# An LSTM mixture behind windowed attention: the cell's work a gate unit later, halves stored as pairs, and the output projection with features on partitions

## What is computed

```python
h = tok(x)                                   # embedding (89 columns) beside a short-time spectrum (39)
h = h + attn(layernorm(h)) @ W_out + b_out   # 8 heads of 16; 64 summary tokens and windows of 17
n = layernorm(h)
top2 = top_k(n @ router_w + router_b, 2)     # weights: a softmax over the two
# every expert e is an LSTM over the 16 steps, for both choices k and all 512 tokens:
gates = (mask[k, e] * n) @ Wi[e] + hid @ Wh[e] + b[e]      # i, f, g, o
c = sigmoid(f) * c + sigmoid(i) * tanh(g)
hid = sigmoid(o) * tanh(c)
out = h + sum over k, e of mask[k, e] * weight[k] * (hid @ Wo[e] + bo[e])
```

## Time and profile before

| what | value |
|---|---|
| time, median of 3 runs | 1915.93 us (1915.46 to 1918.11) |
| the profiled execution | 1918.11 us |
| its span, first to last instruction | 1916.3 us |
| PE busy | 1729.1 us, 90% |
| DVE busy | 1559.5 us, 81% |
| ACT busy | 991.9 us, 52% |
| POOL busy | 65.2 us, 3% |
| granted TensorE clock, mean | 0.970 |

### The profile page before, as it was taken

One profiled execution on the slowest core, in us unless ns is written; L12 is line 12 of the kernel. 1 busy time (PEld: TensorE's weight loads), 2 busy tenths in 40 slices (PEclk: granted clock), 3 DMA queues, 4 the chain that ended last, 5 costly groups with the idle time before them and its releaser, 6 DMA issues.

```text
span 1916.3 us, 25885 instructions
## 1 busy us (share of the span) xinstructions
PE 1729.1 (90%) x9898; PEld 837.6 (44%) x9898; DVE 1559.5 (81%) x2433; ACT 991.9 (52%) x1114; POOL 65.2 (3%) x42
## 2 busy tenths in 40 slices
PE   3457799999999999999999999999999999999998
PEld 2223344444444444444444444444444444444443
DVE  2649698897988889798898988889898888979865
ACT  3234554646555555645545455455555555564544
POOL 1000000000000000000000000000000000000000
PEclk9668899999999999999999999999999999999999
DMA  3113241413314132232313224151331413223221
GB/s 114 20 41 74 57 67 46 77 37 67 63 49 74 39 70 52 52 70 51 67 45 69 51 57 67 44 80 37 63 66 46 76 37 71 53 50 67 55 61 36
DMA packets 318594, 110.95 MB, mean 58 GB/s; under 512 B 240331, under 2 KB 299581, under 8 KB 318471
## 3 DMA queue, kind: packets, MB, share of 16 engines
q1 hardware_dynamic: 202758, 101.96, 23.9%
q10 hardware_dynamic: 115712, 7.34, 3.8%
HBM read 89.84 MB, written 4.74 MB: 49 GB/s over the span
## 4 chain that ended last, share of the span: by engine, by line
PE 40%; DVE 33%; DMA 8%; issue 7%; ACT 5%; ACTq 4%; SPq 1%; POOL 0%; DVEq 0%
PE gates L506 25%; ACTq L619 4%; DVE C L1017 4%; DVE tmp L1007 4%; DMA masks<-mask_scratch 3%; DVE tmp L1013 3%; DMA prod<-in_x_ids 3%; DVE xm L985 3%; PE yp L512 3%; DVE Hs L997 3%; DVE tmp L1028 3%; DVE xn L795 2%; PE FA L447 2%; ACT tmp L655 2%; PE FA L459 2%
## 5 line engine op out<-in xcount | busy, mean ns | idle before, releaser
L655 ACT ACTIVATE tmp<-gates,bias_sb 128x1024 f32<-128x1024 f32 x504 | 557.5, 1109 | 558.6 <-PE gates L506 496.1
L506 PE MATMUL gates<-xm,wi_sb 128*128 128x512 f16 x3024 | 747.3, 384 | 46.2 <-ACT tmp L655 31.0
L506 PE MATMUL gates<-Hs,wh_sb 128*128 128x512 f16 x2880 | 704.4, 381 | 0.0
L506 PEld LDWEIGHTS gates<-xm,wi_sb 128*128 128x128 f16 x3024 | 290.3, 99 | 435.3 <-issue 105.1
L506 PEld LDWEIGHTS gates<-Hs,wh_sb 128*128 128x128 f16 x2880 | 283.2, 98 | 344.3 <-issue 8.0
L662 ACT ACTIVATE tmp<-C 128x1024 f32<-128x1024 f32 x128 | 135.2, 1057 | 226.4 <-DVE C L1017 223.2
L992 DVE SCALAR_TENSOR_TENSOR tmp<-tmp 128x1024 f32<-128x1024 f32 x128 | 155.9, 1218 | 71.8 <-ACT tmp L662 71.8
L1007 DVE SCALAR_TENSOR_TENSOR tmp<-tmp 128x1024 f32<-128x1024 f32 x120 | 144.9, 1208 | 46.4 <-ACT tmp L655 44.9
L985 DVE TENSOR_TENSOR xm<-xs,masks 128x2048 f16<-128x2048 f16 x128 | 155.2, 1212 | 32.7 <-DMA masks<-mask_scratch 32.7
L997 DVE SCALAR_TENSOR_TENSOR Hs<-tmp,Hs 128x1024 f16<-128x1024 f32 x120 | 146.4, 1220 | 37.7 <-ACT Hs L666 36.7
L1013 DVE SCALAR_TENSOR_TENSOR tmp<-tmp,C 128x1024 f32<-128x1024 f32 x120 | 146.4, 1220 | 14.4 <-ACT tmp L655 14.0
(11 more groups left out here) (155 smaller groups left out, 1218.9 us busy)
## 6 DMA issues: line engine op xcount, KB each, us to landing
masks<-mask_scratch SPq DMA_DIRECT2D x128, 256.0 KB, 5.0
roww<-mw_scratch SPq DMA_DIRECT2D x128, 256.0 KB, 4.0
rowk<-mask_scratch SPq DMA_DIRECT2D x128, 128.0 KB, 3.0
diag<-pr SPq DMA_DIRECT2D x64, 112.0 KB, 4.3
diag<-vwin ACTq DMA_DIRECT2D x64, 112.0 KB, 4.8
out_dram<-h SPq DMA_DIRECT2D x16, 256.0 KB, 3.7
C<-in_wi SPq DMA_DIRECT2D x1, 2048.0 KB, 10.9
C<-in_wh SPq DMA_DIRECT2D x1, 2048.0 KB, 15.6
```

The source lines that it names most:

```text
L506: last = mm(gates[:, slot, k * SEQ:(k + 1) * SEQ], w, v, start=(i < K), stop=(i >= len(seq) - K))
L655: A(tmp[:, gate_at(gate, e), :], gates[:, (n - 1) % 2, :], ACT.Tanh, bias=bias_sb[:, e, gate:gate + 1], scale=UNSCALE).then_inc(s_tanh, 1)
```

## The change

**Cell work a unit later.** `cell(e)` moves to g = 0 of the following expert, with `cell_tanh` at the same g = 0 (behind the tanh of I), `hidden` to the end of g = 1, `split_hi` to g = 2, `hidden_lo` and `chosen` to g = 3, `input_part` to g = 2. `unit_y` and the bias of y stand at g = 1 instead of g = 0. To let this be, `tmp` has eight planes in place of seven (two for F, two for O), and the product of `chosen` goes to the second half of the O plane instead of a tile `z32`, so that its wait for the last `unit_y` goes and the tanh of O waits for `unit_y` instead. The last cell and cell tanh stand after the loop.

**Pairs of halves.** In `qz`, `vhl`, `vwin` and `diag`, the high and low half of an element stand beside each other. The DMAs move 32-bit elements, DVE transposes v once as 32-bit elements, and the products read the diag tile with a step of two halves.

**Projection.** One product of `wout` with the 512 columns of `attn` at t = 21 (features on partitions), a copy on ACT at t = 21 that adds the bias, and four transposes on PE at t = 22. `moments2`, `xn2`, `x2T`, `logits`, `choice`, `weights` and `maskT` each stand one unit later. `SP_AT`, `MASKS_AT` and `XM_AT` don't change; SP's store of the output stands at t = 10 instead of 9.

The diff, without declarations and setup:

```diff
...
     SP_AT = dict(ids=0, qbd=6, rows=28)
-    PE_AT = dict(emb=1, xT=3, qkv=4, summary=7, window=8, feature=14, values=18, proj=21, x2T=23,
-         logits=24, maskT=27)
-    ACT_AT = dict(h=1, xT=3, qkv=4, split=5, summary=9, window=11, vz=9, pr_hi=15, feature=16, x2T=23,
-          choice=25, maskT=27)
+    PE_AT = dict(emb=1, xT=3, qkv=4, summary=7, window=8, feature=14, values=18, proj=21, projT=22,
+         x2T=24, logits=25, maskT=28)
+    ACT_AT = dict(h=1, xT=3, qkv=4, split=5, summary=9, window=11, vz=9, pr_hi=15, feature=16, proj=21, x2T=24,
+          choice=26, maskT=28)
     DVE_AT = dict(onehot=0, moments=1, xn=2, pw=5, q_lo=5, kv_lo=6, v_win=7, w_max=8, s_max=9, s_sub=10, w_sum=11,
           w_out=12, s_sum=13, s_norm=14, f_max=15, p_lo=16, p_T=16, f_sum=17, f_part=18, attn=19,
-          moments2=21, xn2=22, x_lo=24, choice1=25, choice2=25, weights=26)
+          moments2=22, xn2=23, x_lo=25, choice1=26, choice2=26, weights=27)
     MASKS_AT = 29
...
 Hs = sb("Hs", [P, E, 2, K * SEQ], f16)
-tmp = sb("tmp", [P, 7, K * SEQ])
+tmp = sb("tmp", [P, 8, K * SEQ])
 masks = sb("masks", [P, 2, K, SEQ], f16)
...
 roww = sb("roww", [P, 2, SEQ])
-z32 = sb("z32", [P, SEQ])
...
 oW = sb("oW", [P, NW])
-diag = sb("diag", [P, 2, NBLK, NG, 2 * DH], f16)
+diag = sb("diag", [P, NBLK, NG, 2 * DH])
 vwin = sb("vwin", [P, NBLK * 32])
...
 wT = rows[WT0:WT0 + E, :]
-qz = pr[:, :].bitcast(f16).rearrange("p (v j c q) -> p v j c q", v=2, j=NBLK, c=2)
+qz = pr[:, :].bitcast(f16).rearrange("p (j c q v) -> p j c q v", j=NBLK, c=2, v=2)
...
 pr16, prT16 = pair16(pr[:, :], NBLK * KB), pair16(prT[:, :], NBLK * KB)
-vw16 = vwin[:, :].bitcast(f16).rearrange("p (v j d) -> p v j d", v=2, j=NBLK)
-vhl = ew[:, 0:TF + 2 * PAD].bitcast(f16).rearrange("p (v t) -> p v t", v=2)
+vwj = vwin[:, :].rearrange("p (j d) -> p j d", j=NBLK)
+vp = ew[:, 0:TF + 2 * PAD]
+vp16 = pair16(vp, TF + 2 * PAD)
 khl = xn[:, :, :].rearrange("p t d -> p (t d)").bitcast(f16)[:, 0:2 * (TF + 2 * PAD)] \
...
-    return {I: e % 2, G: 2 + e % 2, F: 4, O: 5 + e % 2}[gate]
-
-TANH_C = gate_at(F, 0)
+    return {I: 0, G: 2, F: 4, O: 6}[gate] + e % 2
+
+def chosen_at(e):
+
+    return tmp[:, gate_at(O, e), SEQ:2 * SEQ]
...
 fid = tmp[0:NFFT, 2, 512:512 + NBJ].bitcast(i32)
-diag_flat = diag[:, :, :, :, :].rearrange("p v j g d -> p (v j g d)")
-onehot64 = diag_flat[0:NFFT, 2 * VOCAB * NBJ:3 * VOCAB * NBJ]
-mag = diag_flat.bitcast(f32)[0:NFREQ, 0:VOCAB * NBJ]
+diag_flat = diag[:, :, :, :].rearrange("p j g d -> p (j g d)")
+diag16 = diag_flat.bitcast(f16).rearrange("p (j m v) -> p j m v", j=NBLK, v=2)
+onehot64 = diag_flat.bitcast(f16)[0:NFFT, 2 * VOCAB * NBJ:3 * VOCAB * NBJ]
+mag = diag_flat[0:NFREQ, 0:VOCAB * NBJ]
 dft_sb = tmp[0:NFFT, 2, 0:2 * NFREQ]
...
             for g in range(NG):
-                load(diag[32 * g:32 * g + 32, :, :, g, :].rearrange("p v j d -> p (v j) d"),
-                     qz[32 * g:32 * g + 32, :, :, :, :].rearrange("p v j c q -> p (v j) (c q)"), S["qbd"])
+                load(diag[32 * g:32 * g + 32, :, g, :],
+                     pr[32 * g:32 * g + 32, :].rearrange("p (j d) -> p j d", j=NBLK), S["qbd"])
         if t == SP_AT["rows"]:
...
             e, g = t // NG, t % NG
-            if t == 9 and not first:
+            if t == 10 and not first:
                 store(s - 1, 1 - par)
...
                     for qv, kv in ((HI, HI), (HI, LO), (LO, HI)):
-                        last = mm(FA[:, r, jj * KB:(jj + 1) * KB], diag[:, qv, j, :, :].rearrange("p g d -> p (g d)"),
+                        last = mm(FA[:, r, jj * KB:(jj + 1) * KB], diag16[:, j, :, qv],
                                   khl[:, kv, j * QB:j * QB + KB], start=False,
...
                 for vv, pv in ((HI, HI), (HI, LO), (LO, HI)):
-                    last = mm(FA[:, j // HB, (j % HB) * KB:(j % HB + 1) * KB], diag[:, vv, j, :, :].rearrange("p g d -> p (g d)"),
+                    last = mm(FA[:, j // HB, (j % HB) * KB:(j % HB + 1) * KB], diag16[:, j, :, vv],
                               prT16[:, j * KB:(j + 1) * KB, pv], start=(vv == HI and pv == HI), stop=(vv == LO))
...
             pe.wait_ge(S["attn"], b1)
+            mm(FA[:, 1, :], wout_sb[:, :], attn[:, :], start=True, stop=True).then_inc(S["projT"], 1)
+        if t == PE_AT["projT"]:
+            pe.wait_ge(S["projS"], b1)
             for i in range(TILES):
-                mm(FB[:, i * D:(i + 1) * D], attn[:, i * P:(i + 1) * P], wout_sb[:, :], start=True, stop=False)
-                last = mm(FB[:, i * D:(i + 1) * D], ones1[:, :], bout_sb[:, :], start=False, stop=True)
+                last = nc.tensor.transpose(FB[:, i * D:(i + 1) * D], xnT[:, i * P:(i + 1) * P], ident[:, :])
             last.then_inc(S["proj"], 1)
...
         pe.wait_ge(s_z, s * E + e + 1)
-        mm(yp[:, :], wo_sb[:, e, :], z32[:, :], start=False, stop=(e == E - 1)).then_inc(s_y, 1)
+        mm(yp[:, :], wo_sb[:, e, :], chosen_at(e), start=False, stop=(e == E - 1)).then_inc(s_y, 1)
...
                 unit_gate(s, e, g, first)
-            if g == 0 and e == 2:
+            if g == 1 and e == 2:
                 y_bias(s)
-            if g == 0 and e >= 2:
+            if g == 1 and e >= 2:
                 unit_y(s, e - 2)
-            elif g == 0 and not first:
+            elif g == 1 and not first:
                 unit_y(s - 1, e - 2 + E)
...
             act.wait_ge(S["v"], b1)
-            A(vhl[:, HI, :], vf[:, :], ACT.Copy, scale=Q_SCALE).then_inc(S["vhi"], 1)
+            A(vp16[:, :, HI], vf[:, :], ACT.Copy, scale=Q_SCALE).then_inc(S["vhi"], 1)
         if t == ACT_AT["summary"]:
...
             for g in range(NG):
-                act.dma_start(diag[32 * g:32 * g + 32, :, :, g, :].rearrange("p v j d -> p (v j) d"),
-                              vw16[32 * g:32 * g + 32, :, :, :].rearrange("p v j d -> p (v j) d")) \
+                act.dma_start(diag[32 * g:32 * g + 32, :, g, :], vwj[32 * g:32 * g + 32, :, :]) \
                     .then_inc(S["vz"], 16)
...
             A(ew[:, 0:TF], prod[:, 0:TF], ACT.Exp).then_inc(S["ef"], 1)
+        if t == ACT_AT["proj"]:
+            act.wait_ge(S["projT"], b1)
+            A(xnT[:, :], FA[:, 1, :], ACT.Identity, bias=bout_sb[:, 0:1]).then_inc(S["projS"], 1)
         if t == ACT_AT["x2T"]:
...
         m = s * E + e
-        if gate == F and m >= 1:
-            act.wait_ge(s_h, m)
+        if gate == F and m >= 2:
+            act.wait_ge(s_h, m - 1)
         elif gate == O and m >= 2:
-            act.wait_ge(s_z, m - 1)
+            act.wait_ge(s_y, m - 1)
         elif m >= 2:
...
         act.wait_ge(s_c, s * E + e + 1)
-        if s == 0 and e:
-            act.wait_ge(s_h, e)
-        A(tmp[:, TANH_C, :], C[:, e, :], ACT.Tanh, scale=0.5).then_inc(s_tc, 1)
+        if s == 0 and e >= 2:
+            act.wait_ge(s_h, e - 1)
+        A(tmp[:, gate_at(F, e), :], C[:, e, :], ACT.Tanh, scale=0.5).then_inc(s_tc, 1)
...
                 y_out(s - 1)
-            if g == 0 and e and not last:
+            if g == 0 and e:
+                cell_tanh(s, e - 1)
+            elif g == 0 and not first:
+                cell_tanh(s - 1, E - 1)
+            if g == 2 and e and not last:
                 split_hi(s, e - 1)
-            elif g == 0 and not e and not first:
+            elif g == 2 and not e and not first:
                 split_hi(s - 1, E - 1)
-            if g == 3:
-                cell_tanh(s, e)
             if not last:
...
     run_steps(step_p)
+    cell_tanh(STEPS - 1, E - 1)
     y_out(STEPS - 1)
...
             for c in range(2):
-                last = STT(out=qz[:, LO, :, c, :], in0=qT[:, NW:SEQ].rearrange("p (j q) -> p j q", q=QB),
-                           scalar=parq[:, c:c + 1], in1=qz[:, HI, :, c, :], op0=ALU.mult, op1=ALU.subtract)
+                last = STT(out=qz[:, :, c, :, LO], in0=qT[:, NW:SEQ].rearrange("p (j q) -> p j q", q=QB),
+                           scalar=parq[:, c:c + 1], in1=qz[:, :, c, :, HI], op0=ALU.mult, op1=ALU.subtract)
             last.then_inc(S["qlo"], 1)
...
             wait("vhi", b1)
-            STT(out=vhl[:, LO, :], in0=vf[:, :], scalar=Q_SCALE, in1=vhl[:, HI, :],
+            STT(out=vp16[:, :, LO], in0=vf[:, :], scalar=Q_SCALE, in1=vp16[:, :, HI],
                 op0=ALU.mult, op1=ALU.subtract).then_inc(S["vlo"], 1)
...
-            for v in (HI, LO):
-                own = vhl[:, v, :]
-                win = bass.AP(tensor=own.tensor, offset=own.offset, ap=[list(own.ap[0]), [QB, NBLK], [1, KB]])
-                last = V.transpose(vw16[:, v, :, :], win)
-            last.then_inc(S["vwin"], 1)
+            win = bass.AP(tensor=vp.tensor, offset=vp.offset, ap=[list(vp.ap[0]), [QB, NBLK], [1, KB]])
+            V.transpose(vwj, win).then_inc(S["vwin"], 1)
         if t == DVE_AT["w_max"]:
...
         at = tmp[:, gate_at(O, e), :]
-        STT(out=at, in0=at, scalar=1.0, in1=tmp[:, TANH_C, :],
+        STT(out=at, in0=at, scalar=1.0, in1=tmp[:, gate_at(F, e), :],
```

(33 more changed lines are left out.)

18 lines of the change are left out of this document (9 added, 9 removed).

## The result

The changed kernel takes 1992.63 us (median, 1990.79 to 1993.24) against 1917.02 for the kernel before in the same runs: a ratio of 1.0392, interval 1.0374 to 1.041. It is 75.6 us slower; the forecast was 14 slower. The prediction was wrong, in size though not in sign, and its range (1870 to 1950) doesn't hold the time. The span of its profiled execution is 1991.4 us at a mean granted clock of 0.942; before, it was 1916.3 at 0.970.

What follows compares the result with a forecast made beforehand. TensorE work took 107 of 114 us a step, the rest mostly ends of chains through other engines. 14 steps x 1.7 gave +24, front -6.5, step 0 -3: net +14.5 on 1915.9, so 1930 us, range 1870 to 1950.

Steps and rivals of the forecast that it cites:

- The way around a step's end: From the projection's start to the next step's first gate unit: 37.5 us against 35.2, +2.3 us a step.
- The way from t0 to the projection: From a step's first gate unit to its projection: -0.6 us a step, embedding delay and smaller terms included.
- The stops at t11 and t17: PE's stops of 0.9 and 1.6 us for ACT's tanh go: -2.5 us a step.
- the value products 0.25: In a step's first stretch, the value products lose 0.25 us.
- 41.4 us of work from the end of v's transposes to the end of attn: DVE's work there, less two waits of 2.8 us together; walked to attn done 76.8 us after the first gate unit.
- Front and step 0: The front before step 0 shortens by 6.5 us, step 0 by 3 us, both as bare chains.
- The pairs: DVE gains 1.0 us a step, diag DMA issues cost 0.65 us each, products with stepped stationary operands cost nothing more.
- The projection: PE work falls by 1.9 us a step; ACT's copy ends 0.6 us after PE would want it.
- Lost in waiting: The 1.9 us a step saved in PE by the new projection are lost in waiting at the step's end.
- weights with a step load slower: Rival: stationary operands with a step load at half rate or worse, 1997 us and up; chance 0.08.
- DVE would be early enough: Rival: second norm no later than now, h2 to xn2's end under 5.9 us, 1898 or 1866 us; chance 0.25.
- gains and losses cancel: Rival: ACT's wait for the cell moves from unit 3 to unit 0, all within 0.2%, 1916 us; chance 0.08.

Runs made afterwards that it cites:

- high_half_early: The changed kernel with ScalarE making the high half of a hidden in the second unit of a gate set, not the third: 1957.72 us, ratio 1.02.
- fill_stops: The changed kernel with products that do nothing useful put ahead of four waits of TensorE: 1981.68 us, ratio 1.0323.
- chosen_rows_first: The changed kernel with DVE building the chosen input of expert 6 ahead of the next step's first masked input: 1958.59 us, ratio 1.0201.
- orders_no_norm: The changed kernel with mask rows copied before the cell tanh, expert 6's chosen input before the masked input, and high half a unit earlier: 1876.5 us, ratio 0.9788.
- pairs_orders: The kernel before with pairs of halves, mask rows copied before the high half, and chosen input before the masked one; old projection: 1880.89 us, ratio 0.9792.
- pairs_alone: The kernel before with the halves stored as pairs, nothing else of the change: 1897.46 us, ratio 0.9889.
- norm_first: The changed kernel with xn2 and ACT's copy of its transposes ahead of the cell's calls in their units: 1994.06 us, ratio 1.0385.
- proj_alone: The kernel before with the new projection and its tables, nothing else of the change: 1918.76 us, ratio 0.9994.

## Why the prediction was wrong, step by step

The sign was right and the size wrong by 63 us. By its own steps:

- **The way around a step's end was right.** From the start of the projection to the next t0 it gave 37.5 us against 35.2; the mean over 14 steps is 37.7 against 35.2. Its parts hold too: h2 at 4.65 (4.27), mask rows' copy to t0 8.7 (8.8), stop before the second transposes 1.9 (1.98), embedding 9.2 after t0 (9.23). Of the stop of 3.2 there, 1.7 is filled by the slow unit of t0, so that the low clock costs nothing at that place; what is left of the stop is 0.5 to 1.9, not the "over 2.5 us" that the forecast named as its sign.
- **The way from t0 to the projection was wrong.** It gave 0.6 us less; it grew from 78.7 to 81.8, so +3.1. This is 3.7 of the 3.9 us a step by which the forecast is short. The stops at t11 and t17 went as forecast (-2.5; t11 to t17 fell by 2.48). What failed is the step "the value products 0.25": t18 takes 1.95 more (1.7 of these 3.7). The walk let DVE do its "41.4 us of work from the end of v's transposes to the end of attn" without a pause but the two waits it had, and the change put into it a low half that waits for ACT. I had counted the high half's move (g = 2) in the list of moves and named nobody who waits for it. `high_half_early` shows the price: 35 us in all.
- **A second step is missing, the clock.** The forecast priced gate units behind a stop at 2.60 us everywhere. In many steps they were at the low clock: t2 behind stops of 1.1 to 1.9 us (+1.24 on average), t19 behind one of 1.76 (+1.0), t25 behind one of 1.98. With the missed part of t18 that makes 1.7 + 1.24 + 1.0 = 3.9 against the 3.7; t3 to t10 fell by 0.9, which is 0.3 more than forecast. `high_half_early` and `chosen_rows_first` show that the cause is the stop: take it away and t19 or t2 is at the full clock in every step (in `high_half_early` t19 still takes 0.4 more than before, in a stop of about 0.5 for ACT's tanh). But these figures of the walk aren't what the clock costs. `fill_stops` gives it back at t0, t19 and t25 and is 11 us faster, the added products included, for t1 waits longer in exchange. And in `chosen_rows_first`, where t2 is fast, t3 to t10 take 0.65 us more than in the changed kernel, so of the 1.24 at t2 about half is won.
- **Front and step 0.** -5.7 for -6.5 is right; step 0 gained nothing (+1.4 for -3). It is 96.9 in the best kernel with the cell late (`orders_no_norm`), 95.0 with the norm first as well, and 92.5 with the cell in place, the same projection and the same pairs. With the cell in place and the old projection (`pairs_orders`) it is 96.7. So the gain that the forecast took for step 0 comes from the new projection (4.2 us), but only with the cell in its old place; which call holds it up, I didn't follow.
- **The pairs**: the steps hold. DVE is busy 16.4 us less in `pairs_alone` (1543.1), 1.0 a step; the products cost nothing, the stop of 0.9 at t11 gone. DMA issue on ACT, taken at 0.65, has a median of 0.69 (from 1.02); in the changed kernel (columns as there):

```profile
L626 ACTq DMA_DIRECT2D diag<-vwin x64: 592/686/1577, 71.4 to 1810.9; - x64
```

- **The projection**: PE -1.9 holds, the copy ends 0.6 late (stop of 0.42). "Lost in waiting" was right for the copy's order as it stood and wrong as a rule: with two calls swapped the projection is worth 19.5 us, though even there the period falls by 1.06 and not by 1.9.
- **The rivals.** That weights with a step load slower is refuted by the blocks of 2.25 and 2.27 us. That DVE would be early enough: the embedding and the second norm were late as the forecast said, so its condition (h2 to the end of xn2 under 5.9 us) wasn't met: in the step shown h2 starts at 1134.65 and PE begins on xn2 at 1141.77, 7.1 us later (6.95 by the forecast's walk). That gains and losses cancel was wrong, though its mechanism is real: ACT's wait for the cell is still there, 255.0 us.

The range ended at 1950, since "1 us a step either way" was taken for the own error of a walk of 100 instructions over three engines, in which one missed wait costs 2 us a step, 28 in all, and pulls the clock with it.

## What to carry to other kernels

When an instruction is moved, list not only what it waits for but everything that waits for it, on every engine, and look what stands before each of those in its queue; a half that is made on another engine (here the high half) is such a waiter. When two chains end at the same point, an experiment with one of them can show nothing (2.7 us and 34 us here), and both, with a third order beside them, show 80: try orders together, and price a saving (here the projection: 0 or 19.5 us) only when what it stands behind is known. Before work is moved to another unit, swap calls inside a unit: it adds no work, and two swaps brought 16.6 us (1897.5 to 1880.9). Not every swap pays: `norm_first` took 7 us beside the others.

## What the runs showed of the hardware

- Behind a stop TensorE often took up its work at the lower clock level, and the length of the stop alone doesn't tell whether. In the changed kernel, over 14 steps: t0 was low in all 14 behind stops of 2.6 to 3.7 us (4.27 us for a unit and not 2.60, granted clock 0.60), t19 in 10 behind one of 1.76, t2 in 10 behind stops of 1.1 to 1.9, t25 in 4 behind one of 1.98, t29 never behind one of 0.9 to 1.1. In `proj_alone` t0 was low in 8 behind stops of 2.3 to 2.6 (once 6.4) and at the full clock in 6 behind stops of 2.5 to 3.3.
- The clock also fell without a stop: in the kernel before, right behind the eight short f32 products of the projection, in 4 of 14 steps (granted clock 0.59 of the next unit, 1.00 of the products).
- A block of 84 products whose stationary operand is f16 with a step of two halves takes 2.25 to 2.27 us, as with a dense one (2.25). The Trainium skill, "TensorE: Matmul & The Clock Gate", section "Weight-path perf modes", has 32-bit reads and a strided pattern in one table; the runs bear out the second, for no load of these blocks got slower.
- With runs of 128 bytes in place of 64, packets fell from 318594 to 204045, the median issue on ACT from 1.02 to 0.69 us and the time from issue to landing from 4.8 to 3.1 us.
